# Rows scattered behind the next image's router chain, from four buffers in the last weights' place

## The reference, cut to what matters

```python
x = x + conv0(ln_c(x))            # router picks 2 of 4 experts for each image, 3x3 convolutions, plus a shared 1x1
t = to_tokens(x)
t = t + ffn0(ln_t(t))             # each of 16384 tokens goes to 2 of 8 experts, hidden 341, gated
x = from_tokens(t)
x = x + conv1(ln_c(x))            # 3x3 depthwise, weights computed from the image's mean
t = to_tokens(x)
t = t + ffn1(ln_t(t))             # each token goes to 1 of 8 experts with a capacity, hidden 512
out = from_tokens(t)
```

## Time and profile before

| | us |
|---|---|
| median of three executions | 2282.22 |
| lowest, highest | 2279.48, 2284.02 |
| span of the profiled execution | 2530.8 |
| busy in it: TensorE, VectorE, ScalarE, GpSimd | 1850.5, 1499.0, 1020.8, 1003.1 |
| its 384 scatters at L588, busy | 387.2 |

### The profile page before, as it was taken

How to read it: one execution, slowest core, us unless ns; L and a number is a source line. 1 busy time by engine, 2 the same in 40 slices (tenths; PEclk the granted TensorE clock), 3 DMA queues, 4 the chain that set the end, 5 groups by cost and what they waited for, 6 DMA issues and landing times.

```text
span 2530.8 us, 39768 instructions
## 1 busy us (share of the span) xinstructions
PE 1850.5 (73%) x8630; PEld 970.6 (38%) x8631; DVE 1499.0 (59%) x5297; ACT 1020.8 (40%) x1718; POOL 1003.1 (40%) x1180
## 2 busy tenths in 40 slices
PE   0487776777767754999999994988888856888823
PEld 0343332333333322444444442554554433444412
DVE  2766554555545543777677773555555545777768
ACT  0433232332323322666666663434333323555411
POOL 0002344333443343665565564133333323665510
PEclk9788888788887876999999997988888867999955
DMA  9200101001010013222222222111111003222134
GB/s 269 78 17 26 35 33 34 27 26 34 32 34 28 18 39 79 70 67 68 69 65 69 67 69 59 56 51 50 50 51 50 16 16 87 67 68 65 46 116 149
DMA packets 180056, 148.97 MB, mean 59 GB/s; under 512 B 19302, under 2 KB 161822, under 8 KB 179960
## 3 DMA queue, kind: packets, MB, share of 16 engines
q1 hardware_dynamic: 153336, 98.05, 13.8%
q0 software_dynamic: 26624, 49.93, 5.6%
HBM read 76.00 MB, written 77.34 MB: 61 GB/s over the span
## 4 chain that ended last, share of the span: by engine, by line
PE 29%; issue 26%; DVE 16%; another core or an unknown queue 12%; ACT 7%; SPq 5%; DMA 3%; POOL 2%; ACTq 1%; DVEq 0%; POOLq 0%
PE banks L892 7%; PE banks L694 5%; PE banks L695 5%; PE banks L696 5%; PE banks L689 3%; ACT work L980 3%; PE banks L707 3%; SPq L478 2%; SPq L407 1%; DVE small L1282 1%; DMA work<-slot_rows 1%; SPq L479 1%; POOL ffn_rows L609 1%; DVE small L1167 1%
## 5 line engine op out<-in xcount | busy, mean ns | idle before, releaser
L609 POOL DMA_INDIRECT ffn_rows<-work x448 | 469.4, 1048 | 354.2 <-issue 201.8
L588 POOL DMA_INDIRECT slot_rows<-work,small x384 | 387.2, 1008 | 543.8 <-DVE small L1454 422.1
L689 PE MATMUL banks<-small,work 128*128 128x128 f32 x1920 | 301.2, 295 | 276.5 <-ACT work L980 87.9
L689 PEld LDWEIGHTS banks<-small,work 128*128 128x128 f32 x1920 | 242.5, 152 | 385.1 <-issue 187.5
L892 PE MATMUL banks<-work 128*128 128x512 f32 x576 | 301.3, 671 | 0.9 <-DVE work L1716 0.9
L694 PE MATMUL banks<-work,wb_h 128*128 128x512 f16 x648 | 247.2, 382 | 29.9 <-issue 17.7
L1660 DVE TENSOR_TENSOR work<-work 128x512 f16<-128x512 f32 x376 | 259.0, 689 | 12.6
L695 PE MATMUL banks<-work,wb_h 128*128 128x512 f16 x648 | 245.8, 379 | 0.0
L696 PE MATMUL banks<-work,wb_l 128*128 128x512 f16 x648 | 245.8, 379 | 0.0
L694 PE MATMUL banks<-work,wa_h 128*128 128x512 f16 x576 | 241.0, 418 | 3.5 <-ACT work L1011 3.2
L695 PE MATMUL banks<-work,wa_h 128*128 128x512 f16 x576 | 241.4, 419 | 0.0
(11 more groups left out here) (243 smaller groups left out, 2987.7 us busy)
## 6 DMA issues: line engine op xcount, KB each, us to landing
work<-slot_rows SPq DMA_DIRECT2D x112, 264.0 KB
work<-ffn_rows SPq DMA_DIRECT2D x48, 512.0 KB, 4.2
ffn_rows<-small SPq DMA_DIRECT2D x32, 256.0 KB, 3.8
work<-in_x SPq DMA_DIRECT2D x16, 512.0 KB, 3.3
out_image<-work SPq DMA_DIRECT2D x16, 512.0 KB, 2.6
ffn_rows<-work POOLq DMA_INDIRECT x448
slot_rows<-work,small POOLq DMA_INDIRECT x384
slot_rows<-small SPq DMA_DIRECT2D x17, 264.0 KB, 4.0
```

The lines of the kernel that those rows point to most:

```text
L588: pool_e.indirect_dma_start(slots, bass.IndirectOffsetOnAxis(ap=slot_i[:, row_buffer(p, i, k), tt:tt + 1], axis=0), rows[row_buffer(p, i, ...
L609: pool_e.indirect_dma_start(dst, bass.IndirectOffsetOnAxis(ap=idg[old.v][:, qq, 0:1].bitcast(I32), axis=0), yt[old.u][:, qq, :], None, bou ...
L689: last = pe.transpose(dst[:, tt * P:(tt + 1) * P], x, ident)
```

## The change

The 16 scatters of image i - 2 now wait for `A_hb` of image i + 1 too, where that image exists. Rows of stage A get four buffers (two choices, two parities of the image), in place of two; the semaphores that count their scatters are split in the same way, and `route_rows` and the copy L1055 wait for the scatters of the image two before. The four buffers lie in the SBUF space of the ffn1 weights, now one tile `late` of 32 KB in each of 128 partitions. So SyncE stores `late` to HBM before it loads the first images, ScalarE waits for the store before stage A, SyncE loads it back after the last tile load of stage B, and TensorE waits for that before stage D. Stages B to F keep their buffers. `slot_i` has four entries in place of two.

```diff
@@ buffers
-        wd1_h = sb("wd1_h", [P, E * HID1], F16)      (and wd1_l, wd2_h, wd2_l)
+        late = sb("late", [P, 4 * E * HID1 // 2])
+        wd1_h, wd1_l, wd2_h, wd2_l = (late[:, k * (E * HID1 // 2):(k + 1) * (E * HID1 // 2)].bitcast(F16) for k in range(4))
+        tL = carve(late)
+        rows_a = [[tL([TPI, ROW]) for _ in range(2)] for _ in range(2)]
         def row_buffer(p, i, k):
-            return k if p == "A_" else i.u
+            return rows_a[i.u][k] if p == "A_" else rows[i.u]
+        def row_lane(p, i, k):
+            return f"{k}{i.u}" if p == "A_" else f"{i.u}"
@@ SyncE
             sp.wait_ge(sem("setup_done"), 1)
+            sp.dma_start(parked_late, late[:, :]).then_inc(sem("late_parked"), 16)
             x_img = a["x"].rearrange("b c h w -> b c (h w)")
...
             tile_loads("B_", TILES0, "A_", 2)
+            sp.dma_start(late[:, :], parked_late).then_inc(sem("late_parked"), 16)
@@ GpSimd
             def a_step(i):
+                nxt = i + 1
+                if live(i + (-2), IMAGES) and live(nxt, IMAGES):
+                    pool_e.wait_ge(sem("A_hb"), nxt.b + 1)
                 scatters("A_", i + (-2), 2)
-                nxt = i + 1
                 if live(nxt, IMAGES):
@@ TensorE
+            pe.wait_ge(sem("late_parked"), 32)
             ffn("D_", TILES1, NJ1, False, (wd1_h, wd1_l), None, (wd2_h, wd2_l))
@@ ScalarE
-                earlier = i.b if p == "A_" else i.h
-                if some(earlier):
-                    act.wait_ge(sem(f"{p}scattered_rows{buf}"), earlier * (16 * TPI))
+                if some(i.h):
+                    act.wait_ge(sem(f"{p}scattered_rows{row_lane(p, i, 0)}"), i.h * (16 * TPI))
...
-                    if some(old.b):
-                        act.wait_ge(sem("A_scattered_rows1"), old.b * (16 * TPI))
-                    act.activation(rows[1][:, :, 0:C], rows[0][:, :, 0:C], ACT.Copy).then_inc(sem("A_rows2_ready"), 1)
+                    if some(old.h):
+                        act.wait_ge(sem(f"A_scattered_rows1{old.u}"), old.h * (16 * TPI))
+                    act.activation(rows_a[old.u][1][:, :, 0:C], rows_a[old.u][0][:, :, 0:C], ACT.Copy).then_inc(sem("A_rows2_ready"), 1)
+            act.wait_ge(sem("late_parked"), 16)
             sweep(act, IMAGES, a_step)
@@ VectorE
-                first = 0 if choices == 2 else i.u
+                first = 2 * i.u if choices == 2 else i.u
                 dve.tensor_copy(slot_i[:, first:first + choices, :], slot_f[:, 0:choices, :]).then_inc(sem(p + "slots_known"), 1)
```

More of the change, by code:

```diff
@@ L166, in build @@
     parked = nc.dram_tensor("conv1_weights", (P, (1 + TAPS) * P), F32, kind="Internal").ap()
+    parked_late = nc.dram_tensor("ffn1_weights", (P, 4 * E * HID1 // 2), F32, kind="Internal").ap()
     back1 = nc.dram_tensor("ffn1_rows", (TOKENS, C), F32, kind="Internal").ap()
@@ L197, in build @@
         wb2_l = sb("wb2_l", [P, E * NJ0 * C], F16)
-        wd1_h = sb("wd1_h", [P, E * HID1], F16)
-        wd1_l = sb("wd1_l", [P, E * HID1], F16)
-        wd2_h = sb("wd2_h", [P, E * NJ1 * C], F16)
-        wd2_l = sb("wd2_l", [P, E * NJ1 * C], F16)
+        late = sb("late", [P, 4 * E * HID1 // 2])
+        wd1_h, wd1_l, wd2_h, wd2_l = (late[:, k * (E * HID1 // 2):(k + 1) * (E * HID1 // 2)].bitcast(F16) for k in range(4))
         work = sb("work", [P, 11800])
-        small = sb("small", [P, 2800])
+        small = sb("small", [P, 2816])
         def carve(tensor):
@@ L281, in build @@
         idf = t([TPI])
-        slot_i = t([2, TPI], I32)
+        slot_i = t([4, TPI], I32)
         hg = t([1])
@@ L467, in tile_loads @@
                 sp.wait_ge(sem("zeroed"), 16 * (TOKENS // TILE + 1))
-                for k in range(2):
-                    sp.wait_ge(sem(f"{before}scattered_rows{k}"), 16 * NT * choices // 2)
+                if choices == 2:
+                    for lane in ("00", "01", "10", "11"):
+                        sp.wait_ge(sem(f"A_scattered_rows{lane}"), 16 * NT // 2)
+                else:
+                    for lane in ("0", "1"):
+                        sp.wait_ge(sem(f"C_scattered_rows{lane}"), 16 * NT // 2)
                 def load_tile(i):
@@ L588, in scatters @@
                         pool_e.indirect_dma_start(
-                            slots, bass.IndirectOffsetOnAxis(ap=slot_i[:, row_buffer(p, i, k), tt:tt + 1], axis=0),
-                            rows[row_buffer(p, i, k)][:, tt, :], None, bounds_check=SLOTS - 1, oob_is_err=False
-                        ).then_inc(sem(f"{p}scattered_rows{row_buffer(p, i, k)}"), 16)
+                            slots, bass.IndirectOffsetOnAxis(ap=slot_i[:, 2 * i.u + k if choices == 2 else i.u, tt:tt + 1], axis=0),
+                            row_buffer(p, i, k)[:, tt, :], None, bounds_check=SLOTS - 1, oob_is_err=False
+                        ).then_inc(sem(f"{p}scattered_rows{row_lane(p, i, k)}"), 16)
             def tile_step(p, i, n, dst, limit):
@@ L699, in route_turn @@
                 pe.wait_ge(sem(p + "rows_ready"), i.b + 1)
-                turn(tp, [rows[row_buffer(p, i, 0)][:, tt, 0:C] for tt in range(TPI)]).then_inc(sem(p + "nT_done"), 1)
+                turn(tp, [row_buffer(p, i, 0)[:, tt, 0:C] for tt in range(TPI)]).then_inc(sem(p + "nT_done"), 1)
             def logits(p, i, w):
@@ L986, in route_rows @@
                 buf = row_buffer(p, i, 0)
-                earlier = i.b if p == "A_" else i.h
-                if some(earlier):
-                    act.wait_ge(sem(f"{p}scattered_rows{buf}"), earlier * (16 * TPI))
+                if some(i.h):
+                    act.wait_ge(sem(f"{p}scattered_rows{row_lane(p, i, 0)}"), i.h * (16 * TPI))
                 apart(act)
                 tok = lambda tt: tokens[:, bass.ds(i.b * TPI + tt, 1), :].rearrange("p a c -> p (a c)")
-                normalise(p, i, lambda tt: rows[buf][:, tt, 0:C], tok, row_stats, "rows_ready")
+                normalise(p, i, lambda tt: buf[:, tt, 0:C], tok, row_stats, "rows_ready")
             def route_copy(p, i):
@@ L1385, in route_place @@
                 dve.wait_ge(sem(p + ("rows2_ready" if choices == 2 else "rows_ready")), i.b + 1)
-                bufs = [rows[row_buffer(p, i, k)] for k in range(choices)]
+                bufs = [row_buffer(p, i, k) for k in range(choices)]
                 for k, buf in enumerate(bufs):
                     dve.tensor_scalar(buf[:, :, C], idf, float(k * TOKENS), None, ALU.add)
-                    if isinstance(i.b, int) and i.b < 3 - choices:
+                    if isinstance(i.b, int) and i.b < 2:
                         dve.memset(buf[:, :, C + 2:ROW], 0.0)
```

## The result

The changed kernel takes **2316.7 us** (median of 4 runs, 2313.81 to 2318.71) against 2283.1 us before (4 runs): a ratio of 1.0147, 95% interval [1.0132, 1.0161]. It is slower by 33.6 us. Forecast were 2278 us and a range of 2225 to 2302; time and sign are both missed. Three runs of the experiments were disturbed and are left out of the ratios: 2559.37 and 6616.98 us in e3, 2376.52 in e17; without them the medians given there, 2285.09 and 2289.42, would be 2284.54 and 2289.33.

The account below looks back on a forecast made before the run. Each step of stage A was seen standing still about 11 us at the router's silu, but only when profiled. Store +14, row buffers -18, moved burst 0: -4 from 2282.2 gives 2278 us, range 2225 to 2302.

Parts of the forecast that it names:

- The stall: Stage A: ScalarE's router silu idles until the scatter burst ends, 137 us in the profile; taken as worth nothing when timed.
- The second sign: VectorE's dependent steps lag (idle 0.54) during bursts beside convolutions, 0.20 us where TensorE is idle; read as recording cost.
- the first rival: Silu's stall also in timed executions: a third removed gives 2232 us, the whole 2141; chance 0.22.
- the row wait: Stage A: route_rows waits for earlier scatters; removing this gains 1.0 us in each of 12 steps, 12 us.
- The store: Start: storing 4.19 MB of ffn1 weights ahead of the first images delays stage A, cost 14 us.
- The four buffers: Stage A: route_rows no longer waits for the latest scatters, gain 18 us including the last two steps.
- The two last steps: End of stage A: route_rows starts 2.5 and 3.7 us behind the statistics, a wait the four buffers remove.
- The 12 steps: Stage A: ScalarE loses 1.0 us per step waiting for scatters, on the path; gain 12 us.
- the third rival: Stage A's row wait was hidden behind TensorE, leaving 4 us of gain: +10, 2292 us; chance 0.17.
- The burst moved: Stage A: scatters begin behind A_hb, GpSimd's addition L623 starts 5 us later, no one waits for it: 0 us.
- The rival of the other sign: Stage A: real stall follows the moved burst onto group mean, row logits and gates; 20 us lost, 2298; chance 0.15.

Follow-up runs that it names:

- e3: Changed kernel without GpSimd's wait on A_hb (store and four buffers kept, burst in its old place): 2285.09 us, ratio 1.0004 to before.
- e17: Changed kernel with GpSimd's addition between the tenth and eleventh scatter, on a first-kind chip: 2289.42 us, ratio 1.0026 to before.
- e1: Kernel before, unchanged, profiled again on a first-kind chip: 2283.44 us, ratio 0.9997.
- e2: Kernel before plus only the store and load back of the ffn1 weights (two row buffers, burst in its old place): 2297.7 us, ratio 1.0055.
- e9: Changed kernel, unchanged, on a second-kind chip: 2556.07 us, ratio 1.0058 to before.
- e16: Kernel before with only GpSimd's addition delayed into VectorE's chain of small steps, on a first-kind chip: 2324.64 us, ratio 1.0177.
- e6: Kernel before with only GpSimd's addition made to wait for A_gn_read2, on a second-kind chip: 2533.4 us, ratio 0.9988.
- e7: Changed kernel without the wait on A_hb, store behind the first two image loads, on a second-kind chip: 2538.57 us, ratio 1.0015 to before.
- e11: Repeat of e6 (kernel before, only the addition delayed) on a second-kind chip: 2545.27 us, ratio 1.0016.
- e12: Repeat of e7 (no wait on A_hb, store behind two image loads) on a second-kind chip: 2545.89 us, ratio 1.0023 to before.
- e14: Repeat of e6 (kernel before, only the addition delayed) on a second-kind chip: 2533.31 us, ratio 0.9998.
- e13: Repeat of e5 (changed kernel, addition between tenth and eleventh scatter) on a second-kind chip: 2466.63 us, ratio 0.9746 to before.
- e5: Changed kernel with GpSimd's addition between the tenth and eleventh scatter, on a second-kind chip: 2464.72 us, ratio 0.9728 to before.
- e8: Changed kernel with the addition between tenth and eleventh scatter and the store behind two image loads, second-kind chip: 2459.27 us, ratio 0.9697 to before.
- e10: Repeat of e5 (changed kernel, addition between tenth and eleventh scatter) on a second-kind chip: 2479.92 us, ratio 0.9765 to before.
- e15: Repeat of e8 (addition between scatters, store behind two image loads) on a second-kind chip: 2462.47 us, ratio 0.9722 to before.
- e18: Repeat of e8 (addition between scatters, store behind two image loads) on a second-kind chip: 2473.05 us, ratio 0.9736 to before.

## Why the prediction was wrong

*The stall.* "I therefore take the silu's stall as a cost of the recorded execution, close to nothing in the timed ones": false in its reason. The stall is as real in timed runs as in the profile, on one kind of chip (timed 2535 to 2542 against the span of 2530.8), and absent from both on the other (e1). The 248.6 us between span and median were not the price of recording; by all that these runs show, the two numbers came from different chips. From silu 0 to silu 15 alone the execution of the earlier trace rows takes 741.4 us where e1's takes 566.8, so 174.6 us of the difference lie there, more than the 137 that the list of waits gave. The second sign, the lag of 0.54 us, is absent from e1's recorded execution too, so it was no sign of recording. On the chip of the timed runs there was nothing to win, so the term was right there by luck: the first rival, "the stall is in the timed executions too", is not what happened. Behind it stood a premise that I never wrote down: that profile and median describe one machine. It cost the sum nothing here, as the term was taken as zero, but it made the first rival possible and had the row wait worked out from rows with the lag. The rule of the Trainium skill ("NOTIFIC — the notification-queue block", section "Overflow: three behaviours, one of which stalls the engine") that I set beside it may hold, but it is no account of this stall: e1 was recorded in the same way, with the same 39768 instructions, and does not have it.

*The store.* +14 forecast, 13.5 measured (e2). The method, bytes by the rate of the setup's loads, holds for the transfer: 13.7 forecast, 12.3 in the row. That the whole term fits so well is partly luck. The prediction wanted the first image at TensorE about 14 us later, and it came 9.8 later: the store was issued 0.5 us earlier than the image before (106.20, 106.70), and the image follows the store's landing by 1.5 us (119.99 less 118.5), where it took 3.5 from its own issue. The other 3.5 us of e2 came in stage B and behind it, where no term of the sum lies.

*The four buffers.* -18 forecast, -12.6 measured (e3 against e2), and differently composed. The two last steps were to give 6 and give 8.8. The 12 steps were to give 1.0 each and give nothing. The wait itself was read about rightly: in before on the first kind the scatters are listed as releaser of `route_rows` in 12 steps, the last three among them, and in the nine others it starts 1.1 to 1.7 us behind the end of the statistics, in after and e3 0.3. One such row, timeline of before on the first kind; it is 3.0 us behind the silu at 417.88, in after 2.2 us (480.75 less 478.51):

```profile
420.92 3.19 ACT L980 ACTIVATE work<-tokens,small 128x128 f32 x8 [2.79 <-DMA slot_rows<-work,small]
```

What failed is "It is on the path": the rows start earlier and the stretch is no shorter, 567.7 us in e3, 567.1 in e2, 566.8 in before. This is the third rival, "The row wait was hidden". Its sum was +10 for store and buffers together; e3 measured +0.9, since the two last steps gave more than its 4 and the start cost less than 14.

*The burst moved.* This is the step that failed: "Behind it on GpSimd stands L623 ... it would start 5 us later ... nothing." The addition starts 24.8 us behind the silu (503.26 less 478.51) where it was 16.7, so 8 us later and not 5, since `A_hb` comes at 481.8 and the burst 4.2 us behind the silu, not 0.5; nobody waits for its result. I asked only who needs its output, and not what it does to its neighbours while it runs. It lasts 2.37 us, and until it ends VectorE is held at one small instruction of its chain. In before this fell where VectorE reads PSUM or waits for TensorE; in after it falls into a run of small dependent steps, in 12 of the steps between silu 0 and silu 15. The 12 held instructions (2.48 to 3.06 us each) last 34.3 us together instead of some 12 x 0.18; that is 32 us, for +26.2 in that stretch. The term was to be 0 and is +31.6 in the medians (27.2 in the profiled spans of after and e3).

The Trainium skill bears on this directly, and I had cited it on the wrong side: "SBUF — State Buffer", section "Who interferes with whom", gives VectorE's second pair of ports to GpSimd as well. A VectorE instruction with two SBUF inputs, or in a two-port mode, then contends with a GpSimd instruction that reads SBUF, and whoever issues first keeps the pair for its whole length; one with at most one SBUF input outside those modes does not. I had weighed only VectorE holding the scatters, which would have left the sum as it was. The traces agree with the other direction: 3.05 us for a tensor_scalar of 0.16 and 2.28 for a scalar_tensor_tensor of 0.21, while the statistics read from PSUM beside the same addition keep their 0.70 and 1.67, and an aggregate with one SBUF input its 0.21. Two things stay open. Whether the held tensor_scalar, which has one SBUF input, was in a two-port mode, no trace shows; and in after its record starts up to 0.65 us ahead of the addition's, so that by recorded starts the one that came first was the one held. The scatters themselves do not stretch: they are 1.28 us apart in after as in before.

*The rival of the other sign* had a right mechanism on the wrong chips. "The stall is real but follows the burst": on the second kind just that happens, and it lands on the row logits (e9), for a net +0.58%. On the first kind there is no stall to follow, and that its 2298 lies on the right side of before is chance.

*The sum, with the sizes measured:* +13.5 - 12.6 + 31.6 = +32.5, and 2284.2 + 32.5 = 2316.7. It closes by construction, as the last term is the difference of two medians; that e17 removes 27.3 of it and e16 brings 41.5 of the same sort without moving a scatter is what shows its cause. The remaining 4 us (e17 against e3) are not shown to be the scatters' own: of the 2.9 us between those two profiled spans, 2.4 lie in stage B and behind it, and the stretch with the moved bursts is 0.7 us shorter.

## What to carry to other kernels

When work is moved on a queue, everything behind it moves too; ask of each such instruction not only who waits for its result, but which engine it locks out while it runs, and look at what that engine does at the new place. When a profile's span and the median of the timed runs differ by more than the spread of the runs, find out whether both come from the same chip before explaining the difference by anything in the program.

## What the runs showed of the hardware

- Beside a GpSimd tensor_tensor on 128x1024 f32 in SBUF (2.34 to 2.38 us), one small VectorE instruction (SBUF to SBUF, 1 to 64 elements per partition; tensor_scalar, scalar_tensor_tensor, tensor_tensor or a cast were seen) lasts until the addition ends: 2.3 to 3.1 us instead of 0.15 to 0.22 when it starts with the addition or up to 0.65 us ahead of it, 0.38 to 1.38 when it starts while the addition runs. Statistics read from PSUM (0.70) and a BATCH_NORM_AGGREGATE in SBUF (0.21) run beside it at their usual length.
- One kernel, two times. Beside bursts of 16 indirect DMAs, an instruction that waits for TensorE is released on the second kind only about when the burst ends, in stage A after 10.3 to 12.6 us of idle time on average: the silu in the first profile and in e6, e7, e11, e12 and e14, the row logits in e9. On the first kind the silu follows after 0.99 us, and no list of waits has a "remote" entry. What distinguishes the two is open. On the second kind, with a break of 2.4 us in the burst, filled by the addition, the wait on the row logits is 83.9 us in all in place of 163.8, and the kernel takes 0.9746 of before in place of 1.0058 (e13 and e9, different chips; the wait is 84.6 to 86.4 in e5, e8, e10, e15 and e18); that the break is the reason was not tested apart from the addition's new place. The better version of one kind is thus not that of the other: e5's is 2.4 to 2.7% faster than before on the second and 0.26% slower on the first.
